# The backward scan's D times x joins the forward sum as a TensorE product with a diagonal matrix, in a two-layer Mamba block

## The chip, the cores and the metric

The kernel runs on one core of one Trainium2 chip. The metric is the device time of one execution in microseconds, here the median of three runs. In the profile the engines are PE (TensorE), DVE (VectorE), ACT (ScalarE), POOL (GpSimd) and SP (SyncE, which issues the DMAs).

## The reference

The input x has 8 images of 96 channels and 32 x 32 places. Two layers follow each other. Each is a Mamba block with 192 inner channels and 16 states; the core of it is

```python
def step(h, inp):
    x_t, dt_t, B_t, C_t = inp
    dA = jnp.exp(dt_t[:, :, None] * A)
    h = dA * h + dt_t[:, :, None] * B_t[:, None, :] * x_t[:, :, None]
    y = jnp.einsum('bds,bs->bd', h, C_t)
    return (h, y)
...
return jnp.swapaxes(ys, 0, 1) + x * D
...
return y * _silu(z) @ W_out
```

where x is the silu of a causal convolution of four taps over an input projection, dt is a softplus, and B and C come from a projection of x. Layer 0 runs it along each row of 32 places and normalises the result over the channels. Layer 1 normalises again and runs it over all 1024 places of an image, once forward and once on the flipped sequence, with the same weights, and adds the two outputs. The gate silu(z) and W_out are the same in both directions, so the kernel adds the two y before the gate. The term x * D occurs in each direction: it is D times the forward x plus D times the backward x, and the two x differ, since the convolutions run opposite ways.

## The kernel before

**Items, tiles, steps.** The images go in four pairs. A pair has three items: ROWS (layer 0), FWD and BWD (layer 1). The 192 channels of two images are three tiles of 128 partitions x 1024 places: tile 0 and tile 1 are the first 128 channels of either image, tile 2 holds the last 64 channels of both. A tile has 16 states, so an item has 48 steps. The twelve items stand in the order ROWS 0, ROWS 1, FWD 0, BWD 0, ROWS 2, FWD 1, BWD 1, ROWS 3, FWD 2, BWD 2, FWD 3, BWD 3, and make 576 steps.

**A step** g works on one state of one tile. ACT computes the decay exp(delta*A) of 128 x 1024 (L616). The input u*B is made in one of two ways: PE spreads a row of B over the partitions into b_ps (L479, `look_ahead`) and DVE multiplies it by u there (L771), with the decay in a_ring; or, for the steps listed in BY_POOL, SP fetches the spread row into b_ring by DMA, POOL multiplies it (L850), and the decay goes into b_ps. DVE then scans (L805) into one of 6 slots of `ring`. POOL multiplies the slot by a row of C that a DMA has spread into c_ring (L856, `product`), and PE adds it to y_ps in PSUM by a product with the identity, half by half (L487, `sum_half`), accumulating over the 16 states. When a tile is summed, DVE's `take` (L785) adds y_ps, half by half, to yv in SBUF.

**Order.** Each engine walks the steps in an order of its own (`walk`): PE ahead, sum_0, jobs, sum_1; ACT the decays ahead, then jobs; DVE take_0, scan, take_1, ahead, jobs; POOL the b product of step g+3, then product g, then jobs; SP the b rows of step g+6, the c rows of step g+3, then jobs. PE's sums run 4 steps late (SUM_LAG), so walk step s sums step s-4, and the scan of step g waits for the sums up to step g-6 (RING). SP's fetch of a b row waits for the scan that read the slot before; b_ring has 2 slots. In `take` a tile is taken at walk step 4 of the next tile.

**Jobs** are the rest of the work, put by hand into slots (the step numbers in PREP, POST, FIRST_BACK and so on), in order on every engine. The preparation of the next item: convolution on PE (xr_first and xr, L534), silu into xs on ACT (L653), the projection dbl on PE (L510), its split into three bf16 parts on ACT and DVE (L665, L666, L673, L830, L834), the DMAs bc_in of SP (L408 to L419), dt on PE with softplus on ACT (L678), and u on POOL (L866, L868). The work behind an item: gated on POOL (L877), w_out on PE, and for ROWS also centre, var, log, rstd, norm (L881) and affine. PE, ACT and DVE hand results over through `bank`, two halves of PSUM of which each has to be emptied before it is used again.

**skip** is the job of the term x * D. For ROWS and FWD, ACT writes xs * D into yv (L656), which starts the sum in SBUF. For BWD the job stands in FWD's steps 14, 16 and 16 (12, 14 and 17 for the first pair, FIRST_BACK), and DVE adds xs * D to FWD's yv with one scalar_tensor_tensor per tile of 128 x 1024 (L824); all its operands lie in SBUF. `take` of the forward tile waits for both signals of skip_done. xs holds the x of one item; the silu of the item after BWD writes over BWD's.

**constants** is a job before the first step: DVE splits the weights of dt, corrects w_out (L754), makes w_centre (L756) and at last negates neg_a (L759), for which PE's next job waits through s_const.

Of the kernel before, what the change touches and what calls it, by code (L numbers as in the profile page):

```python
# [8 lines left out]
B, C, H, W = 8, 96, 32, 32  # L9
T = H * W  # L10
DI = 2 * C
NS = 16
RANK = C // 16
TAPS = 4
P = 128
# [9 lines left out]
TILES = 3  # L25
# [53 lines left out]
SUM_LAG = 4  # L79


def fills_prep(kind, pair, at=None):
# [7 lines left out]
    for k in range(TILES):  # L90
        out.append((at["skip"][k], "skip", k))
# [120 lines left out]
def build_program(nc, x, wpack, out):  # L212
# [6 lines left out]
    with ExitStack() as ctx:  # L219
# [24 lines left out]
        w_centre = sb("w_centre", [C, C])  # L244
        b_centre = sb("b_centre", [C, 1])
        w_sum = sb("w_sum", [P, 2])
        ring = sb("ring", [P, RING, T])
# [4 lines left out]
        neg_a = sb("neg_a", [P, 2, 2 * NS])  # L252
# [10 lines left out]
        ident = col("ident")  # L263
        small = [col("small", l).rearrange("p (m c) -> p m c", m=2) for l in range(2)]
# [195 lines left out]
        def _(pe):  # L460
# [21 lines left out]
            def sum_half(g, j):  # L482
                n = g % NS
                pe.wait_ge(g_ready, g + 1)
                if n == 0:
                    wait(pe, y_taken, 2 * (g // NS - 1) + j + 1)
                nc.tensor.matmul(half(y_ps[:, :], j), ident, half(ring[:, g % RING, :], j),  # L487
                                 start=(n == 0), stop=(n == NS - 1)).then_inc(g_summed, 1)
# [53 lines left out]
            def job(name, kind, pair, i, unit):  # L542
# [44 lines left out]
                elif name == "centre":  # L587
                    pe.wait_ge(norm_done, 4 * pair + k + 1)
                    product(unit, C, [(w_centre[:, :], half(x1[:, k, :], j))])
# [9 lines left out]
        def _(act):  # L599
# [40 lines left out]
            def job(name, kind, pair, i, unit):  # L640
# [3 lines left out]
                if name == "silu":  # L644

                    if ordinal[kind, pair] and j == 0:

                        before = ITEMS[ordinal[kind, pair] - 1]
                        act.wait_ge(K["set_ready"][before["kind"]], 3 * before["pair"] + nth(k))
                    u = unit_for(name, kind, pair, i)  # L650
# [3 lines left out]
                elif name == "skip" and kind != BWD:  # L654
# [58 lines left out]
        def _(dve):  # L713
# [13 lines left out]
            def constants():  # L727
# [28 lines left out]
                nc.vector.tensor_scalar(w_centre[:, :], col("centre")[0:C, :], col("ln")[0:C, 0:1], None, ALU.mult)  # L756
# [16 lines left out]
            def take(tile, j):  # L773
# [3 lines left out]
                if j == 0:  # L777
                    dve.wait_ge(K["skip_done"][kind], 3 * pair + k + 1)
                    if kind == FWD:
                        dve.wait_ge(K["skip_done"][BWD], 3 * pair + k + 1)  # L780
# [32 lines left out]
            def job(name, kind, pair, i, unit):  # L813
# [3 lines left out]
                if name == "constants":  # L817
                    constants()
                elif name == "skip" and kind == BWD:

                    dve.wait_ge(K["skip_done"][FWD], 3 * pair + i + 1)
                    landed(dve, "silu", kind, pair, 2 * i, 2 * i + 1)
                    y = yv_of(kind, pair, i)
                    nc.vector.scalar_tensor_tensor(out=y, in0=xs[:, i, :], scalar=sm[:, m_of(i), 6:7], in1=y,  # L824
# [125 lines left out]
```

## Time and profile before

| | us |
|---|---|
| median of 3 runs | 2148.76 |
| lowest, highest | 2145.57, 2149.55 |
| the profiled execution's own time | 2145.41 |
| its span, first to last instruction | 2143.4 |
| mean granted clock of TensorE | 0.94 of full |

The profile shows one execution. A group by line gives the busy time of all instructions of one line, engine and form. A timeline gives them in order of time, neighbours of one group merged (x4 is four instructions), and in brackets how long the engine was idle before and which instruction ended that; "<-issue" is a wait for nothing that the profile shows. A product of 32-bit numbers stands in the trace as two MATMUL records. Idle time of an engine that sets no pace costs nothing.

### The profile page before, as it was taken

To read this page: it belongs to the slowest core of one execution; us is meant where nothing else is said; L and a number is where in the kernel's file an instruction comes from. 1 tells how busy PE (TensorE), PEld (TensorE's weight loads), DVE (VectorE), ACT (ScalarE), POOL (GpSimd) and SP (SyncE) were. 2 spreads that over 40 slices of the span, in tenths; PEclk is the share of its full clock that TensorE was granted. 3 is DMA by queue.
4 is the path that set the end of the run, shared out by engine and by line. 5 is a ranking of instruction groups with operands and counts; after the bars stand their busy time and mean duration, and the time that the engine had idled before them with its cause. 6 is when DMAs were issued, how large, how long until landed. Compare 5 with 4: busy or idle time off the path is not lost. (4 is left out here: it accounts for less than half of the span.)

```text
span 2143.4 us, 16030 instructions
## 1 busy us (share of the span) xinstructions
PE 1796.1 (84%) x4426; PEld 693.7 (32%) x4426; DVE 1872.9 (87%) x1120; ACT 1163.1 (54%) x1206; POOL 1944.8 (91%) x852
## 2 busy tenths in 40 slices
PE   5797889887898889789889889879879878877777
PEld 2233233332333333233333333323333333223332
DVE  2888887887899988998899997998989998999994
ACT  2756465645746645644756745745575564453331
POOL 0998999888999999998999999899899999899996
PEclk9798999999999999999999989999999999988897
DMA  3567466536575767665665775685566576667673
GB/s 76 207 214 189 162 224 182 168 147 217 152 213 192 215 188 243 191 200 199 199 177 203 236 207 200 203 207 184 190 186 210 199 214 188 221 200 205 229 213 92
DMA packets 124454, 414.99 MB, mean 194 GB/s; under 512 B 18557, under 2 KB 22925, under 8 KB 124365
## 3 DMA queue, kind: packets, MB, share of 16 engines
q1 hardware_dynamic: 124364, 413.98, 63.4%
q8 instruction: 35, 0.57, 0.1%
q14 instruction: 55, 0.44, 0.1%
HBM read 403.48 MB, written 6.29 MB: 191 GB/s over the span
## 5 line engine op out<-in xcount | busy, mean ns | idle before, releaser
L856 POOL TENSOR_TENSOR ring<-ring,c_ring 128x1024 f32<-128x1024 f32 x576 | 1344.6, 2355 | 93.3 <-DVE ring L805 71.7
L487 PE MATMUL y_ps<-ring,wp 128*128 128x512 f32 x2304 | 1175.9, 628 | 48.0 <-DVE yv_fwd L785 25.6
L805 DVE TENSOR_TENSOR_SCAN ring<-a_ring,b_ps 128x1024 f32<-128x1024 f32 x392 | 895.4, 2284 | 32.3 <-ACT a_ring L616 2.3
L487 PEld LDWEIGHTS y_ps<-ring,wp 128*128 128x128 f32 x2304 | 451.0, 200 | 529.9 <-issue 415.3
L805 DVE TENSOR_TENSOR_SCAN ring<-b_ps,b_ring 128x1024 f32<-128x1024 f32 x184 | 417.2, 2273 | 59.3 <-POOL b_ring L850 31.3
L616 ACT ACTIVATE a_ring<-delta_ab,neg_a 128x1024 f32<-128x1024 f32 x240 | 271.8, 1140 | 183.8 <-DVE ring L805 183.2
L850 POOL TENSOR_TENSOR b_ring<-u_ab,b_ring 128x1024 f32<-128x1024 f32 x144 | 343.7, 2387 | 27.3 <-DMA b_ring<-b_rows 27.3
L771 DVE TENSOR_TENSOR b_ps<-u_ab,b_ps 128x1024 f32<-128x1024 f32 x240 | 290.9, 1212 | 79.3 <-PE b_ps L479 72.8
L616 ACT ACTIVATE b_ps<-delta_ab,neg_a 128x1024 f32<-128x1024 f32 x144 | 160.6, 1116 | 238.8 <-DVE ring L805 238.4
L609 ACT ACT_TABLE_LOAD x186 | 238.6, 1283 | 88.2 <-DVE ring L805 36.0
L616 ACT ACTIVATE a_ring<-delta_m,neg_a 128x1024 f32<-128x1024 f32 x152 | 173.6, 1143 | 154.1 <-DVE ring L805 153.8
L479 PE MATMUL b_ps<-b_in,sel 96*128 96x512 bf16 x480 | 154.8, 407 | 94.9 <-DVE ring L805 93.8
L534 PE MATMUL bank<-x,w_conv 96*128 96x512 f32 (+12 forms) x576 | 205.2, 600 | 5.7 <-ACT xs L653 4.5
L771 DVE TENSOR_TENSOR b_ps<-u_m,b_ps 128x1024 f32<-128x1024 f32 x152 | 183.8, 1209 | 15.3 <-PE b_ps L479 15.3
L479 PE MATMUL b_ps<-b_in,sel_m 96*128 96x512 bf16 x304 | 98.8, 408 | 115.8 <-DVE ring L805 115.6
L479 PEld LDWEIGHTS b_ps<-b_in,sel 96*128 96x128 bf16 x480 | 42.3, 102 | 259.4 <-DVE ring L805 149.9
L534 PEld LDWEIGHTS bank<-x,w_conv 96*128 96x128 f32 (+1 forms) x576 | 71.6, 163 | 126.9 <-issue 112.2
L479 PEld LDWEIGHTS b_ps<-b_in,sel_m 96*128 96x128 bf16 x304 | 24.6, 104 | 235.2 <-DVE ring L805 189.4
L850 POOL TENSOR_TENSOR b_ring<-u_m,b_ring 128x1024 f32<-128x1024 f32 x40 | 95.2, 2380 | 2.1 <-DMA b_ring<-b_rows 2.1
L616 ACT ACTIVATE b_ps<-delta_m,neg_a 128x1024 f32<-128x1024 f32 x40 | 44.7, 1117 | 96.2 <-DVE ring L805 96.2
L534 PE MATMUL bank<-io,w_conv 96*128 96x512 f32 (+5 forms) x192 | 67.0, 596 | 13.8 <-DMA io<-x 13.4
L868 POOL TENSOR_TENSOR u_ab<-delta_ab,xs 128x1024 f32<-128x1024 f32 x8 | 18.8, 2350 | 55.1 <-ACT delta_ab L678 55.1
(76 smaller groups left out, 967.8 us busy)
## 6 DMA issues: line engine op xcount, KB each, us to landing
c_ring<-c_rows SPq DMA_DIRECT2D x384, 512.0 KB, 4.9
c_ring<-c_rows SPq DMA_DIRECT2D x384, 256.0 KB, 4.3
b_ring<-b_rows SPq DMA_DIRECT2D x144, 512.0 KB, 5.2
b_ring<-b_rows SPq DMA_DIRECT2D x80, 256.0 KB, 5.2
out<-io SPq DMA_DIRECT2D x16, 192.0 KB, 5.2
io<-x SPq DMA_DIRECT2D x6, 384.0 KB, 7.1
b_in<-parts SPq DMA_DIRECT2D x36, 64.0 KB, 2.0
dt_in<-parts SPq DMA_DIRECT2D x72, 24.0 KB
```

What stands on the lines that cost most here:

```text
L479: last = nc.tensor.matmul(half(b_ps[:, g % 2, :], j), pick(k, n), half(b_in[:, parity(kind, pair), :], j), start=True, stop=True)
L487: nc.tensor.matmul(half(y_ps[:, :], j), ident, half(ring[:, g % RING, :], j), start=(n == 0), stop=(n == NS - 1)).then_inc(g_summed, 1)
L534: last = nc.tensor.matmul(o, w, m, start=(d == 0), stop=(d == TAPS - 1))
L609: nc.scalar.preload_act_table_set(name)
L616: nc.scalar.activation(dst, delta_of(kind, pair, k), ACT.Exp, scale=neg_a[:, LAYER[kind], m_of(k) * NS + n:m_of(k) * NS + n + 1]).then_inc ...
L771: nc.vector.tensor_tensor(b, u_of(kind, pair, k), b, ALU.mult).then_inc(b_used, 1)
L805: nc.vector.tensor_tensor_scan(out=h, data0=a, data1=b, initial=0.0, op0=ALU.mult, op1=ALU.add).then_inc(h_ready, 1)
L850: nc.gpsimd.tensor_tensor(b, u_of(kind, pair, k), b, ALU.mult).then_inc(b_made, 1)
L856: nc.gpsimd.tensor_tensor(r, r, c_ring[:, g % C_RING, :], ALU.mult).then_inc(g_ready, 1)
L868: nc.gpsimd.tensor_tensor(u, d, xs[:, i, :], ALU.mult).then_inc(u_done, 1)
```

## The change

The DVE job skip for BWD is gone. In its place DVE makes, once among the constants, two matrices of 128 x 128 with D of layer 1 on the diagonal (w_skip). In every FWD tile PE multiplies them with the backward xs, half by half, and accumulates into y_ps ahead of the sum of state 10 (SKIP_AT), that is at walk steps 14, 30 and 46 of the item. `take` waits for ACT's part alone. ACT's silu of the item after BWD waits, tile by tile, for the sums of the forward tile, since these now read the backward xs. To make room, w_centre and neg_a lie in the packed weights wp and are written in place; DVE waits for PE's product of `constants` before it writes over w_centre.

```diff
--- before.py
+++ after.py
@@ -77,6 +77,7 @@
 LEAD = {"ahead": 1, "ahead_c": C_LEAD, "ahead_a": 2, "ahead_a2": 1, "ahead_b": 3}
 SP_LEAD = dict(LEAD, ahead_b=B_LEAD)
 SUM_LAG = 4
+SKIP_AT = 10
 
 
 def fills_prep(kind, pair, at=None):
@@ -87,8 +88,9 @@
         out.append((at["xr"][u], "xr_first", u))
         out.append((at["xr"][u] + 1, "xr", u))
         out.append((at["silu"][u], "silu", u))
-    for k in range(TILES):
-        out.append((at["skip"][k], "skip", k))
+    if kind != BWD:
+        for k in range(TILES):
+            out.append((at["skip"][k], "skip", k))
     for j in range(2):
         for n, name in enumerate(("dbl", "split_hi", "split_mid", "split_lo")):
             out.append((at["dbl"][j] + n, name, j))
@@ -241,15 +243,14 @@
         parts3 = sb("parts3", [SPLIT_ROWS, 2, 3, HALF], bf16)
         dt_in = sb("dt_in", [DT_ROWS, T], bf16)
         w_dt = sb("w_dt_parts", [DT_ROWS, 2, 3, P], bf16)
-        w_centre = sb("w_centre", [C, C])
         b_centre = sb("b_centre", [C, 1])
         w_sum = sb("w_sum", [P, 2])
+        w_skip = sb("w_skip", [P, 2, P])
         ring = sb("ring", [P, RING, T])
         c_ring = sb("c_ring", [P, C_RING, T])
         a_ring = sb("a_ring", [P, A_RING, T])
         b_ring = sb("b_ring", [P, B_RING, T])
         eps = sb("eps", [C, 1])
-        neg_a = sb("neg_a", [P, 2, 2 * NS])
         b_ps = ps("b_ps", [P, 2, T])
         y_ps = ps("y_ps", [P, T])
         bank = ps("bank", [P, 2, HALF])
@@ -261,6 +262,9 @@
             return wp[:, at:at + n]
 
         ident = col("ident")
+        w_centre = col("centre")[0:C, :]
+        at = _cols["a_log", 0][0]
+        neg_a = wp[:, at:at + 4 * NS].rearrange("p (l n) -> p l n", l=2)
         small = [col("small", l).rearrange("p (m c) -> p m c", m=2) for l in range(2)]
         ordinal = {(it["kind"], it["pair"]): n for n, it in enumerate(ITEMS)}
         parity = lambda kind, pair: ordinal[kind, pair] % 2
@@ -484,6 +488,10 @@
                 pe.wait_ge(g_ready, g + 1)
                 if n == 0:
                     wait(pe, y_taken, 2 * (g // NS - 1) + j + 1)
+                kind, pair, k, _ = step_at(g)
+                if kind == FWD and n == SKIP_AT:
+                    landed(pe, "silu", BWD, pair, 2 * k + j)
+                    nc.tensor.matmul(half(y_ps[:, :], j), w_skip[:, m_of(k), :], half(xs[:, k, :], j), start=False, stop=False)
                 nc.tensor.matmul(half(y_ps[:, :], j), ident, half(ring[:, g % RING, :], j),
                                  start=(n == 0), stop=(n == NS - 1)).then_inc(g_summed, 1)
 
@@ -586,7 +594,7 @@
                                       (w[own, C:2 * C], half(yv_of(kind, pair, 2), j)[own, :])])
                 elif name == "centre":
                     pe.wait_ge(norm_done, 4 * pair + k + 1)
-                    product(unit, C, [(w_centre[:, :], half(x1[:, k, :], j))])
+                    product(unit, C, [(w_centre, half(x1[:, k, :], j))])
                 elif name == "var":
                     c = i % 4
                     landed(pe, "w_out" if i < 4 else "centre", kind, pair, c)
@@ -647,11 +655,13 @@
 
                         before = ITEMS[ordinal[kind, pair] - 1]
                         act.wait_ge(K["set_ready"][before["kind"]], 3 * before["pair"] + nth(k))
+                        if before["kind"] == BWD:
+                            act.wait_ge(g_summed, 2 * NS * (TILES * ordinal[FWD, before["pair"]] + k + 1))
                     u = unit_for(name, kind, pair, i)
                     src = full(u)
                     table("silu_and_others")
                     empty(u, nc.scalar.activation(half(xs[:, k, :], j), src, ACT.Silu, bias=sm[:, m_of(k), 4:5]))
-                elif name == "skip" and kind != BWD:
+                elif name == "skip":
                     landed(act, "silu", kind, pair, 2 * i, 2 * i + 1)
                     nc.scalar.activation(yv_of(kind, pair, i), xs[:, i, :], ACT.Identity,
                                          scale=sm[:, m_of(i), 6:7]).then_inc(K["skip_done"][kind], 1)
@@ -724,7 +734,7 @@
             dve.wait_ge(taps_in, 16)
             fold(1)
 
-            def constants():
+            def constants(unit):
                 nc.vector.tensor_copy(sel[:, :, :], col("sel")[0:C, :].rearrange("p (b n) -> p b n", b=2)).then_inc(s_sel, 1)
                 dve.wait_ge(s_sel, 1)
                 for b in range(2):
@@ -753,7 +763,10 @@
                 for v in range(2):
                     last = nc.vector.tensor_scalar(wo[:, v, :], wo[:, v, :], w_sum[:, v:v + 1], None, ALU.add)
                 last.then_inc(s_sums, 1)
-                nc.vector.tensor_scalar(w_centre[:, :], col("centre")[0:C, :], col("ln")[0:C, 0:1], None, ALU.mult)
+                for m in range(2):
+                    nc.vector.tensor_scalar(w_skip[:, m, :], ident, small[1][:, m, 6:7], None, ALU.mult)
+                dve.wait_ge(produced[unit % 2], unit // 2 + 1)
+                nc.vector.tensor_scalar(w_centre, w_centre, col("ln")[0:C, 0:1], None, ALU.mult)
                 dve.wait_ge(s_sums, 3)
                 dve.wait_ge(s_nega, 2)
                 last = nc.vector.tensor_scalar(neg_a[:, :, :], neg_a[:, :, :], -1.0, None, ALU.mult)
@@ -775,9 +788,8 @@
                 it = ITEMS[tile // TILES]
                 kind, pair, k = it["kind"], it["pair"], tile % TILES
                 if j == 0:
-                    dve.wait_ge(K["skip_done"][kind], 3 * pair + k + 1)
-                    if kind == FWD:
-                        dve.wait_ge(K["skip_done"][BWD], 3 * pair + k + 1)
+                    if kind != BWD:
+                        dve.wait_ge(K["skip_done"][kind], 3 * pair + k + 1)
                     if kind == BWD:
                         dve.wait_ge(y_taken, 2 * (tile - TILES + 1))
                 dve.wait_ge(g_summed, 2 * NS * (tile + 1) - 1 + j)
@@ -815,14 +827,7 @@
                 k, j = i // 2, i % 2
                 sm = small[layer]
                 if name == "constants":
-                    constants()
-                elif name == "skip" and kind == BWD:
-
-                    dve.wait_ge(K["skip_done"][FWD], 3 * pair + i + 1)
-                    landed(dve, "silu", kind, pair, 2 * i, 2 * i + 1)
-                    y = yv_of(kind, pair, i)
-                    nc.vector.scalar_tensor_tensor(out=y, in0=xs[:, i, :], scalar=sm[:, m_of(i), 6:7], in1=y,
-                                                   op0=ALU.mult, op1=ALU.add).then_inc(K["skip_done"][kind], 1)
+                    constants(unit)
                 elif name == "split_hi":
                     u = unit_for("dbl", kind, pair, i)
                     dve.wait_ge(K["hi_ready"][kind], 2 * pair + i + 1)
```

## Rows read from the trace of the kernel before

**Rows 1.** The page's first part: busy us, share of the span and xinstructions

```profile
PE 1796.1 (84%) x4426; PEld 693.7 (32%) x4426; DVE 1872.9 (87%) x1120; ACT 1163.1 (54%) x1206; POOL 1944.8 (91%) x852
```

**Rows 2.** Groups by line: xcount | busy us, mean ns | idle before, releasers

```profile
L824 DVE SCALAR_TENSOR_TENSOR yv_fwd<-xs,wp,yv_fwd 128x1024 f32<-128x1024 f32 x9 | 33.5, 3733 | 0.0
...
L824 DVE SCALAR_TENSOR_TENSOR yv_rows<-xs,wp,yv_rows 128x1024 f32<-128x1024 f32 x3 | 13.1, 4392 | 0.0
```

**Rows 3.** Timelines of F3: start us, us, instruction [idle before <-releaser]

```profile
1842.30 10.66 DVE L824 SCALAR_TENSOR_TENSOR yv_rows<-xs,wp,yv_rows 128x1024 f32<-128x1024 f32 x1
...
1855.66 2.27 DVE L805 TENSOR_TENSOR_SCAN ring<-b_ps,b_ring 128x1024 f32<-128x1024 f32 x1
...
1846.38 1.88 PE L487 MATMUL y_ps<-ring,wp 128*128 128x512 f32 x4
...
1862.79 2.41 POOL L850 TENSOR_TENSOR b_ring<-u_ab,b_ring 128x1024 f32<-128x1024 f32 x1 [5.20 <-DMA b_ring<-b_rows]
```

**Rows 4.** Timeline of DVE in F0

```profile
459.70 10.31 DVE L824 SCALAR_TENSOR_TENSOR yv_fwd<-xs,wp,yv_fwd 128x1024 f32<-128x1024 f32 x1
```

**Rows 5.** Timeline of POOL in F0

```profile
466.61 2.33 POOL L850 TENSOR_TENSOR b_ring<-u_ab,b_ring 128x1024 f32<-128x1024 f32 x1
472.30 2.35 POOL L856 TENSOR_TENSOR ring<-ring,c_ring 128x1024 f32<-128x1024 f32 x1 [3.36 <-DVE ring L805]
478.55 2.40 POOL L850 TENSOR_TENSOR b_ring<-u_ab,b_ring 128x1024 f32<-128x1024 f32 x1 [3.91 <-DMA b_ring<-b_rows]
```

**Rows 6.** Timelines of PE, ACT, DVE and POOL in F1

```profile
997.55 4.45 PE L487 MATMUL y_ps<-ring,wp 128*128 128x512 f32 x10
...
998.72 1.10 ACT L616 ACTIVATE b_ps<-delta_ab,neg_a 128x1024 f32<-128x1024 f32 x1
...
991.41 6.98 DVE L824 SCALAR_TENSOR_TENSOR yv_fwd<-xs,wp,yv_fwd 128x1024 f32<-128x1024 f32 x1
...
1001.09 2.27 DVE L805 TENSOR_TENSOR_SCAN ring<-b_ps,b_ring 128x1024 f32<-128x1024 f32 x1
...
1007.37 2.38 POOL L850 TENSOR_TENSOR b_ring<-u_ab,b_ring 128x1024 f32<-128x1024 f32 x1 [4.35 <-DMA b_ring<-b_rows]
```

**Rows 7.** Timeline of PE in F0

```profile
463.03 1.94 PE L534 MATMUL bank<-x,w_conv 96*64 96x512 f32 x8
...
472.27 1.03 PE L479 MATMUL b_ps<-b_in,sel 96*128 96x512 bf16 x2 [6.25 <-DVE ring L805]
...
474.94 2.93 PE L534 MATMUL bank<-x,w_conv 96*64 96x512 f32 x8
```

**Rows 8.** Stretches: length, busy us (x) of PE, PEld, DVE, ACT, POOL, PEclk, DMA

```profile
472.30:477.80 5.50, 5.50 (x12) 1.53 (x12) 5.50 (x4) 1.12 (x1) 2.34 (x1) 0.57 0.42 116
1054.60:1059.80 5.20, 5.20 (x7) 1.76 (x8) 2.28 (x1) 3.14 (x6) 5.20 (x3) 0.50 0.26 84
...
985.00:1012.00 27.00, 23.72 (x55) 8.16 (x54) 24.78 (x14) 12.50 (x20) 19.29 (x10) 1.00 0.44 152
```

**Rows 9.** Timelines around step 30: F1 (PE, POOL), F0, F2 and F3

```profile
1058.09 1.91 PE L487 MATMUL y_ps<-ring,wp 128*128 128x512 f32 x2
...
1075.49 2.36 POOL L856 TENSOR_TENSOR ring<-ring,c_ring 128x1024 f32<-128x1024 f32 x1 [0.20 <-DVE ring L805]
...
555.49 1.23 DVE L771 TENSOR_TENSOR b_ps<-u_m,b_ps 128x1024 f32<-128x1024 f32 x1 [1.92 <-PE b_ps L479]
...
1580.38 9.28 POOL L856 TENSOR_TENSOR ring<-ring,c_ring 128x1024 f32<-128x1024 f32 x4
...
1906.62 0.60 PE L479 MATMUL b_ps<-b_in,sel_m 96*128 96x512 bf16 x2 [2.99 <-DVE ring L805]
```

**Rows 10.** Timeline of PE near step 46 of F1

```profile
1109.39 0.61 PE L479 MATMUL b_ps<-b_in,sel_m 96*128 96x512 bf16 x2 [1.18 <-DVE ring L805]
```

**Rows 11.** Timeline of PE before the first step, and a group by line

```profile
51.64 1.01 PE L510 MATMUL bank<-dt_in,w_dt_parts 72*128 72x512 bf16 x2 [7.01 <-DVE neg_a L759]
...
L754 DVE TENSOR_SCALAR wp<-wp,w_sum 128x96 f32<-128x96 f32 x2 | 0.4, 268 | 0.0
```

## Prediction

> **What bounds the kernel now.** I read the page first: no engine idles much. POOL is busy 91%, DVE 87%, PE 84% [rows 1]. So the share of busy time decides nothing, and the question is which engine sets the pace in each stretch. I call the twelve items R0, R1, F0, B0, R2, F1, B1, R3, F2, B2, F3, B3 in their order (R rows, F forward, B backward). The removed instruction runs in F0, F1, F2 and F3, at steps 12 to 17.
>
> The groups by line [rows 2] show how odd it is. Twelve additions at L824 keep DVE busy for 33.5 + 13.1 = 46.6 us. The group on yv_rows has three, 13.1 us, and one of them takes 10.66 us [rows 3], so the other two take 1.22 us each. Hence 12 x 1.22 = 14.6 us is work, and 32.0 us is time in which the instruction has started and does not finish. It comes to a long hold on the first addition of each F item (10.31, 6.98 and 10.66 us in F0, F1 and F3 [rows 3, 4, 6]; F2 repeats F1) and a short one on one more in F0.
>
> The timelines of F0 show what holds it. DVE starts L824 at 459.70 and is held until 470.01 [rows 4]. POOL multiplies back to back, and the last of four begins at 466.61 and ends at 468.94 [rows 5]; the addition ends 1.07 us later, about one undisturbed duration. In F1 and F3 it is the same. L824 is the only instruction of the steady loop by which DVE reads two tensors of SBUF; scans, products and L785 have one operand in PSUM. I read this as a path into SBUF that DVE's second operand shares with POOL, and that DVE gets only once POOL has run dry.
>
> Then POOL starves in turn: 3.36 us until DVE's next scan, and 3.91 us for a row of b_ring, which SP may fetch only after a scan has freed the slot [rows 5]. F1 has 4.35 us for the second wait [rows 6], F3 5.20 us [rows 3], F2 lies between.
>
> The Trainium skill (SBUF — State Buffer, Who interferes with whom) has the rule: a DVE instruction with two SBUF inputs contends with a GpSimd instruction that reads SBUF, and the one that issues first keeps the shared pair for its whole instruction. The trace agrees on the pair, and not on the length: by the rule a hold ends with the multiplication then running, 2.4 us at most, where F0's lasts 9.1 us, almost four of them.
>
> **Removed: L824, twelve times.** On DVE at most 46.6 us goes. How much of it reaches the end depends on what is late next, and that is PE. sum_1 of a step stands behind the jobs of its slot in PE's order, and scan g waits for sum g-6.
>
> *F0.* PE idles for 6.25 us until 472.27 [rows 7], waiting for the scan behind the held addition. It then works on at a granted clock of 0.57, mostly the lower level of 1.2 GHz [rows 8]: a broadcast and a sum fill the 2.67 us from 472.27 to 474.94, of which half, 1.3 us, is owed to the clock, and the convolution of eight records takes 2.93 us where the one at 463.03 takes 1.94: 1.0 us. Without the hold PE goes straight on, and its own work sets the pace of the scans behind it. Gain 6.25 + 2.3 = 8.55 us, less the added products of this step.
>
> *F1, F2.* Here PE never stopped before the hold was over: between 985 and 1012 it is busy 23.72 of 27.00 us at clock 1.00 [rows 8]. Step 14 has two w_out and one dbl, and sum_1(10) starts only at 997.55 [rows 6]. Scan 16 needs this sum. So the 6.98 us of hold lie beside PE's work, and scan 16, now at 1001.09, can move only as far as PE allows.
>
> *F3.* Only one w_out precedes: sum_1(10) starts at 1846.38, while scan 16 starts at 1855.66 [rows 3]. PE has more than 8 us of slack.
>
> **Added: 24 products.** Each stands in a trace as two MATMUL records, as the five sums do that make the row of ten at 997.55: 4.45 us, 0.44 a record [rows 6]. A forward tile gets four, 1.8 us, at steps 14, 30 and 46 of an F item, all twelve tiles 21 us (42 us at half the clock).
>
> *Tile 0.* Both go ahead of sum_1(10). F0: 8.55 - 1.8 = 6.8 us gain. F1: sum_1(10) ends at 997.55 + 1.8 + 1.0 = 1000.3; the decay for scan 16, which ran at 998.72 for 1.10 us behind the copies of dbl [rows 6], comes 0.9 later and ends at 1000.7. Scan 16 starts there and not at 1001.09: 0.4 us. The next row of b_ring follows the scan's end by a fixed time, and POOL, which is busy from 1007.37 on without a break of note, moves by the same 0.4. F2 likewise 0.4. F3: the sum ends at 1846.38 + 1.8 + 1.0 = 1849.2, the decay with it at about 1849.6; scan 16 moves from 1855.66 by 6.1 us, and POOL's wait for b_ring, which ends at 1862.79 [rows 3], by as much. Sum 6.8 + 0.4 + 0.4 + 6.1 = 13.7 us.
>
> *Tile 1.* In F1 PE works at clock 0.50 before the broadcast of step 32 [rows 8]; the product ahead of sum_1(26) costs 0.86 a record there (the sum at 1058.09 takes 1.71 us for two until the broadcast at 1059.80). The other stands ahead of an idle stretch and is free. DVE waits for that broadcast, and POOL already waits 0.20 for DVE at 1075.49 [rows 9]: a cost of 1.8 us. In F0 DVE waits 1.92 for the broadcast at 555.49, behind two products: 1.8 us too. In F2 the last of the four products from 1580.38 on starts at 1587.3, 2 us after its scan: covered. In F3 PE idles 2.99 us right before: covered. Were these covers gone, 1.8 us each.
>
> *Tile 2.* PE idles 1.18 us in each of the steps around 46 [rows 10]; of the 1.8 us 0.6 may reach the next broadcast, for which DVE has room. I take nothing, at most 4 x 0.6 us.
>
> **Moved and new waits.** PE's wait for silu, behind which stand sums, jobs and broadcasts, is for work at least six steps old and holds nothing; at worst a silu runs late by one table load and 0.7 us, which no row suggests. ACT's silu behind a backward item waits for the sums of a tile that ended at least eight steps before; queued behind it are decays, and I price it at nothing. take no longer waits for the additions, whose signals are never late. No DMA is added or moved.
>
> **Start.** Two scalings of 128x128 stand on DVE ahead of neg_a, for which PE waits 7.01 us until 51.64 and behind which the first scan hangs [rows 11]. The nearest row is L754 with 268 ns for 96 columns, of which two overlap a little: 0.25 us each, 0.5 us in all, bounds 0.3 and 1.0. DVE's new wait there, for the product that makes b_centre, is for one already done, with nothing but the rest of the constants behind it. neg_a and w_centre in wp change places only.
>
> **Sum.** 13.7 - 3.6 - 0.5 = 9.6 us less, against the profiled execution's own time of 2145.4 us: 2135.8. That execution lies 3.4 us below the median of 2148.8, so the forecast is 2139.2 us.
>
> **Rivals.**
>
> *POOL sets the pace, and gets all its idle time back.* 4 x 3.36 + 3.91 + 4.35 + about 4.7 + 5.20 = 31.6 us. For it: POOL is the busiest engine. Against: in F1 and F2 POOL's second wait hangs on scan 16, that on sum_1(10), and PE has no room. Less 3.6 and 0.5: 2121 us. Chance 0.17. (All 46.6 us of DVE would give 2106; nothing speaks for it.)
>
> *Given back later.* In F0 PE waits for dt_in at step 27. If that transfer were due at a time of its own, F0's gain would be lost, and 2.8 us stay: 2146. Against: SP issues it behind a wait on POOL's products, so it should move along. Chance 0.10.
>
> *The hold is not POOL's doing and stays.* If one multiplication of 2.4 us is POOL's part and the rest lands on the next DVE instruction, F0 keeps 10.31 - 1.22 - 2.4 = 6.7 us of hold and F3 7.0 us, which is their gain; 0.8 - 3.6 - 0.5 makes 3.3 us more, 2152. Against: four holds end with POOL's last multiplication. Chance 0.06. The Trainium skill's rule named above (same page and section), by which a hold cannot outlast one instruction, gives this case.
>
> *Slower: PE's backlog at steps 30 and 46.* There the added records stand ahead of broadcasts for which DVE waits. Eight tiles x four records x 0.86 us at half the clock are 27.5 us; all on the path, against 13.7 gained, make 14.3 us more, 2163. It decides from 13.2 of the 27.5 us on. For it: the clock of 0.50 at step 30. Against: PE's idle time around step 46, and the covers in F2 and F3. Chance 0.07.
>
> **Numbers.** The forecast's chance is 0.60, its own range 2131 to 2144. 0.2%, about what a measurement of this kernel can tell from no change, is 4.3 us. Faster 0.60 + 0.17 = 0.77; within it 0.10 + 0.05 of the staying hold = 0.15; slower 0.08. The range 2120 to 2147 takes in the first three cases and leaves out about 0.13.
>
> **What would show it.** DVE busy some 46 us less and no L824; 24 products of w_skip; POOL's pair of waits near step 15 gone from F0, its first wait shorter than 3.4 us in F3, and still 6 to 7 us in all in F1 and F2; PE without the idle 6.25 us in F0. F0 and F3 shorter by 5 to 6 us each, F1 longer by 1, F2 unchanged. I am wrong if POOL's idle time in F1 or F2 falls by over 4 us (then PE was not the limit), if some other DVE instruction is held for several us, or if DVE's waits for the broadcasts grow by over 10 us.

## The result, and the profile after

The changed kernel takes 2133.3 us (median of 4 runs, 2129.02 to 2136.97), the kernel before 2147.2 us over 4 runs (2145.57 to 2149.55). The ratio is 0.9941, 95% interval 0.9919 to 0.9963: 12.7 us less by the ratio, where 9.6 were forecast. Two repetitions of the same pair, in the experiments, give 0.9948 and 0.9936. The time lies in the range and on the side forecast. The profiled execution has a span of 2135.0 us and a time of its own of 2136.97 us, 8.4 less than that of before on either count.

The page's first part after (busy us, share, xinstructions; against [rows 1]):

```profile
PE 1814.8 (85%) x4474; PEld 705.1 (33%) x4474; DVE 1829.8 (86%) x1110; ACT 1162.8 (54%) x1206; POOL 1938.6 (91%) x852
```

DVE is busy 43.1 us less. The additions' 46.6 us went and 0.5 for two scalings came; no other group of DVE moved by over 0.2 us. The other 3 us are overlap: the page counts time in which two neighbouring instructions overlap once, and the durations added up one by one fall by 45.8 us. PE is busy 18.7 us more. That is 48 new records, which the groups by line show (xcount | busy us, mean ns | idle before), with the scalings beneath. Their 26.4 us count the overlap with the rows beside them: two records are 1.02 us long in the timeline below, and the next row starts after 0.86.

```profile
L494 PE MATMUL y_ps<-xs,w_skip 128*128 128x512 f32 x48 | 26.4, 633 | 0.0
...
L767 DVE TENSOR_SCALAR w_skip<-wp 128x128 f32<-128x128 f32 x2 | 0.5, 278 | 0.0
```

**F0.** The timeline of PE (start us, us, instruction), where [rows 7] had an idle 6.25 us:

```profile
466.11 0.60 PE L483 MATMUL b_ps<-b_in,sel 96*128 96x512 bf16 x2
466.55 1.02 PE L494 MATMUL y_ps<-xs,w_skip 128*128 128x512 f32 x2
467.41 1.02 PE L495 MATMUL y_ps<-ring,wp 128*128 128x512 f32 x2
468.36 1.94 PE L542 MATMUL bank<-x,w_conv 96*64 96x512 f32 x8
470.22 1.13 PE L494 MATMUL y_ps<-xs,w_skip 128*128 128x512 f32 x2
471.19 1.88 PE L495 MATMUL y_ps<-ring,wp 128*128 128x512 f32 x4
473.00 1.93 PE L542 MATMUL bank<-x,w_conv 96*64 96x510 f32 x8
```

PE goes from one item to the next without a gap, and the granted clock is 1.00 where it was 0.57 behind the idle stretch [rows 8]; the convolution of eight records takes 1.93 us and not 2.93 (the row of the stretch: length, then busy us of PE, PEld, DVE, ACT, POOL, clock, DMA share, GB/s):

```profile
466.10:474.00 7.90, 7.90 (x27) 2.83 (x27) 5.17 (x3) 3.51 (x4) 7.90 (x4) 1.00 0.58 194
```

POOL, which in [rows 5] waited 3.36 and 3.91 us here, multiplies from 460.15 to 492.7 with no wait. And the scan behind the second product now waits for the sum, so PE sets the pace, as the forecast had it (timeline of DVE):

```profile
472.34 2.29 DVE L817 TENSOR_TENSOR_SCAN ring<-b_ps,b_ring 128x1024 f32<-128x1024 f32 x1 [1.92 <-PE y_ps L495]
```

**F1 and F3.** The timelines of F1, first PE, then ACT, DVE and POOL:

```profile
991.58 2.82 PE L518 MATMUL bank<-xs,wp 128*96 128x512 f32 x6
994.23 1.02 PE L494 MATMUL y_ps<-xs,w_skip 128*128 128x512 f32 x2
995.09 4.46 PE L495 MATMUL y_ps<-ring,wp 128*128 128x512 f32 x10
...
994.43 0.59 ACT L675 ACTIVATE x_out<-bank 96x512 f32<-96x512 f32 x1 [1.67 <-PE bank L518]
994.92 0.58 ACT L676 ACTIVATE parts<-bank 44x512 bf16<-44x512 f32 x1
995.40 2.14 ACT L624 ACTIVATE b_ps<-delta_ab,wp 128x1024 f32<-128x1024 f32 x2
...
995.53 0.69 DVE L835 TENSOR_TENSOR bank<-bank,parts 44x512 f32<-44x512 f32 x1 [5.83 <-ACT parts L676]
996.54 4.47 DVE L817 TENSOR_TENSOR_SCAN ring<-b_ps,b_ring 128x1024 f32<-128x1024 f32 x2 [0.31 <-ACT b_ps L624]
...
1003.09 2.35 POOL L855 TENSOR_TENSOR b_ring<-u_ab,b_ring 128x1024 f32<-128x1024 f32 x1 [7.95 <-DMA b_ring<-b_rows]
```

The 6.98 us of hold [rows 6] have turned into 5.83 us of waiting. PE comes to dbl behind two w_out, ACT copies its result at 994.43, the decay follows at 995.40 and the scan at 996.54. POOL's two idle stretches, 3.36 + 4.35 = 7.7 us, have become one of 7.95. In F3, where one w_out less precedes:

```profile
1843.89 0.69 DVE L835 TENSOR_TENSOR bank<-bank,parts 44x512 f32<-44x512 f32 x1 [3.77 <-ACT parts L676]
1844.89 2.29 DVE L817 TENSOR_TENSOR_SCAN ring<-b_ps,b_ring 128x1024 f32<-128x1024 f32 x1 [0.31 <-ACT b_ps L624]
...
1852.00 2.35 POOL L855 TENSOR_TENSOR b_ring<-u_ab,b_ring 128x1024 f32<-128x1024 f32 x1 [2.91 <-DMA b_ring<-b_rows]
```

POOL idles 2.91 us here and not 3.36 + 5.20 [rows 3].

The items' lengths, each from its first scan to the first scan of the next, and in brackets the start of scan 16 behind the item's first (worked out from the starts of the scans in each trace, us; the kernels of the columns are told below; after_again is the changed kernel a second time):

```
      before        after         after_again   no_product    add_from_psum  add_late
F0  194.3 (65.1)  189.9 (58.1)  192.4 (58.1)  185.7 (56.4)  187.1          189.5
F1  182.3 (65.5)  181.8 (65.1)  180.7 (65.1)  179.0 (64.2)  178.0          187.1 (64.8)
F2  179.3 (65.3)  179.6 (65.1)  180.0 (65.1)  177.9 (64.2)  180.2          186.4 (64.2)
F3  178.4 (69.1)  171.9 (63.0)  171.9 (63.0)  171.3 (62.4)  171.3          179.3
```

The four F items are 11.1 us shorter together, more than the 8.4 us of the span: R0 and B3, which the change doesn't touch, are 1.8 and 2.9 us longer in this trace (B3 from its first scan to the end of its last). From trace to trace of all kernels R0 lies between 168 and 170.5 us, R1 between 184.8 and 190.1, B3 between 150 and 153.9.

The traces show where this comes from: the granted clock falls to its lower level in short stretches, and these don't lie at the same steps in each trace. In B3 the same six records of PE's sums, behind the same wait for `take`, take 2.81 us before and 5.46 after; then DVE waits for the broadcast behind them, as it did not before (PE before, PE after, DVE after):

```profile
1979.77 2.81 PE L487 MATMUL y_ps<-ring,wp 128*128 128x512 f32 x6 [1.68 <-DVE yv_rows L785]
...
1968.59 5.46 PE L495 MATMUL y_ps<-ring,wp 128*128 128x512 f32 x6 [1.68 <-DVE yv_rows L797]
...
1974.71 1.23 DVE L784 TENSOR_TENSOR b_ps<-u_ab,b_ps 128x1024 f32<-128x1024 f32 x1 [1.65 <-PE b_ps L483]
```

Scans 4 to 8 of B3 take 15.5 us with a clock of 1.00 before, and 17.4 us with 0.80 after; 17.2 and 17.3 in the two repetitions of the changed kernel. In R1, the stretch from scan 6 to 10 takes 16.3 us in every trace with at most 2.1 us at the lower level there, 19.4 and 19.5 in the two with 6.8, and 20.9 and 21.0 in the two with 10.2. Whether the change itself moves these stretches, or chance does, no run here decides. So one item carries an uncertainty of 2 to 5 us by where they fall, and only scan starts close behind an item's first are sharp, most of them to 0.1 us and some to 0.7.

### The profile page after: what moved, and what is told of

Read it like the earlier page. It is cut to its first block and busy times, and to the rows that moved or that the text cites. A ratio compares the mean times of both kernels' runs of the same rounds, so it can differ in the third digit from the quotient of the medians.

```text
span 2135.0 us, 16128 instructions
## 1 busy us (share of the span) xinstructions
PE 1814.8 (85%) x4474; PEld 705.1 (33%) x4474; DVE 1829.8 (86%) x1110; ACT 1162.8 (54%) x1206; POOL 1938.6 (91%) x852
## 5 line engine op out<-in xcount | busy, mean ns | idle before, releaser
L624 ACT ACTIVATE a_ring<-delta_ab,wp 128x1024 f32<-128x1024 f32 x240 | 271.8, 1140 | 183.7 <-DVE ring L817 183.2
L624 ACT ACTIVATE b_ps<-delta_ab,wp 128x1024 f32<-128x1024 f32 x144 | 160.4, 1115 | 213.0 <-DVE ring L817 212.6
L624 ACT ACTIVATE a_ring<-delta_m,wp 128x1024 f32<-128x1024 f32 x152 | 173.6, 1143 | 155.0 <-DVE ring L817 154.7
L784 DVE TENSOR_TENSOR b_ps<-u_m,b_ps 128x1024 f32<-128x1024 f32 x152 | 183.8, 1209 | 20.5 <-PE b_ps L483 20.5
L624 ACT ACTIVATE b_ps<-delta_m,wp 128x1024 f32<-128x1024 f32 x40 | 44.7, 1117 | 95.0 <-DVE ring L817 94.9
```

What stands on the lines that cost most here:

```text
L624: nc.scalar.activation(dst, delta_of(kind, pair, k), ACT.Exp, scale=neg_a[:, LAYER[kind], m_of(k) * NS + n:m_of(k) * NS + n + 1]).then_inc ...
L784: nc.vector.tensor_tensor(b, u_of(kind, pair, k), b, ALU.mult).then_inc(b_used, 1)
```

## The experiments

The runs were made in three groups, each with runs of the kernel before of its own (medians 2145.6, 2147.1 and 2146.2 us); the ratios are against all of these in a group. My theory: the hold is a wait of DVE's second SBUF operand for POOL; what it costs is decided by PE's order of work; the products cost PE about 10 us. The rivals were that the hold costs little anywhere because POOL or a transfer is late regardless; that POOL's idle time is what was won; that the products are free.

### The changed kernel again, twice

> The changed kernel as it is, for a comparison on the same chip. If the first measurement (ratio 0.9941) holds, 11 to 14 us less than the kernel before. F0 about 4.5 us shorter, F3 about 6.5 us, F1 and F2 within 1 us of before.

Measured: 2133.62 us, ratio 0.9948 (0.993 to 0.9965). Scan 16 starts at the same 0.1 us in all four F items as in the first trace. Against before, F3 is 6.5, F0 1.9 and F1 1.6 us shorter and F2 0.7 longer, so F0 and F1 miss what was expected of them. Behind scan 16 of F0 the clock is at its lower level for 27.3 us here and for 20.5 in the first trace.

> The changed kernel as it is, for a comparison with the next three on the same chip. 10 to 14 us less than the kernel before.

Measured: 2133.52 us, ratio 0.9936 (0.9921 to 0.9951). Scan 16 starts at the same 0.1 us in F0 and F2, and 0.6 and 0.2 us later in F1 and F3. Against before, F0 is 4.1, F1 1.6 and F3 6.3 us shorter, F2 1.8 longer.

### The change without its products

```diff
                 if kind == FWD and n == SKIP_AT:
                     landed(pe, "silu", BWD, pair, 2 * k + j)
-                    nc.tensor.matmul(half(y_ps[:, :], j), w_skip[:, m_of(k), :], half(xs[:, k, :], j), start=False, stop=False)
```

> The changed kernel with the 24 products of w_skip left out, so D times the backward x is missing from y. Theory (PE sets the pace at tile 0 of every F item and at tile 1 of F0 and F1): 1.8 us less at tile 0 in each of four items and 1.8 us less at tile 1 in F0 and F1, 10 to 11 us less than the changed kernel, some 23 us less than the kernel before. Rival, PE's products lie beside other work: within 3 us of the changed kernel. Rival, POOL sets the pace everywhere: the same as the changed kernel too, and POOL's idle time in F1 and F2 unchanged.

Measured: 2122.91 us, ratio 0.9891 (0.9866 to 0.9916), which is 10.7 us under the changed kernel: the size expected in sum. The scans say where. At tile 0, scan 16 is 1.7 us earlier in F0 (both products, 1.8 forecast), 0.9 in F1 and F2, 0.6 in F3: there only the product ahead of dbl was in the way, not the second. At tile 1 the lead over the changed kernel grows between scans 28 and 32 by 2.2 us in F0 (from 111.3 - 109.7 = 1.6 to 132.5 - 128.7 = 3.8), and in the same way by 1.6 in F1, 0.8 in F2 and 0.1 in F3. Taken against the two repetitions of the changed kernel it is 1.3 and 2.4 in F0, 1.4 and 0.0 in F1, -0.2 and 0.7 in F2, -0.3 and 0.2 in F3: so far out, the price by item isn't sharp.

### The addition kept, its second operand taken from PSUM

```diff
+    skip = at["skip"] if kind != BWD or at is not PREP else (14, 14, 17)
...
-                    nc.vector.scalar_tensor_tensor(out=y, in0=xs[:, i, :], scalar=sm[:, m_of(i), 6:7], in1=y,
...
+                    dve.wait_ge(b_used, dve_before[g] + 1)
+                    nc.vector.scalar_tensor_tensor(out=y, in0=xs[:, i, :], scalar=sm[:, m_of(i), 6:7], in1=b_ps[:, g % 2, :],
```

> The kernel before, with DVE's addition reading its second operand from b_ps in PSUM instead of yv in SBUF, at steps 14, 14, 17 (so yv gets D times x plus a wrong tile; length, place and count of the instruction are kept). Theory (the hold is a wait for the path into SBUF that POOL uses): no hold, twelve instructions of 1.2 to 1.3 us, DVE busy 32 us less at this line, F0 and F3 shorter by 5 to 7 us each, the whole 9 to 13 us less than before, since DVE's remaining 15 us lie beside PE's and POOL's work. Rival, the hold comes from the instruction itself or its scalar operand: holds of 7 to 11 us stay, and the time is that of before.

Measured: 2121.98 us, ratio 0.9902 (0.9876 to 0.9929). The groups by line of this kernel:

```profile
L828 DVE SCALAR_TENSOR_TENSOR yv_fwd<-xs,wp,b_ps 128x1024 f32<-128x1024 f32 x9 | 11.3, 1279 | 0.9
L828 DVE SCALAR_TENSOR_TENSOR yv_rows<-xs,wp,b_ps 128x1024 f32<-128x1024 f32 x3 | 3.8, 1279 | 0.3
```

Against [rows 2], the same instruction of the same size, takes 15.1 us in place of 46.6. Each of the twelve overlaps a multiplication of POOL, and none is held, nor is any of these multiplications longer than 2.53 us. This shows that the second SBUF operand is what is held. POOL's side was not varied by a run; that it is POOL that holds it rests on the timing, told in the last section. The gain is larger than expected: I had left out that this kernel also doesn't pay for the products, which by the run above are worth 10.7 us. It stands level with the kernel without them.

### The held addition moved to where PE has room

```diff
+    skip = at["skip"] if kind != BWD else (22, 24, 26)
...
-                    if kind == FWD:
-                        dve.wait_ge(K["skip_done"][BWD], 3 * pair + k + 1)
```

> The kernel before, with DVE's three additions of an F item at steps 22, 24 and 26, where PE has slack, and take no longer waiting for them. Theory (in F1 and F2 the hold costs nothing because PE is the limit around step 14): the hold of the first addition stays at 5 to 11 us, now in F1 and F2 too on the path, which become 5 to 8 us longer; F0 and F3 gain at step 14 what they lose at step 22; the whole 8 to 16 us more than before. Rival, a hold costs the same wherever it stands: within 3 us of before.

Measured: 2153.58 us, ratio 1.004 (1.0025 to 1.0055). Timelines of DVE and POOL in F1:

```profile
1018.73 7.14 DVE L823 SCALAR_TENSOR_TENSOR yv_fwd<-xs,wp,yv_fwd 128x1024 f32<-128x1024 f32 x1
1031.49 1.26 DVE L823 SCALAR_TENSOR_TENSOR yv_fwd<-xs,wp,yv_fwd 128x1024 f32<-128x1024 f32 x1
1039.48 2.48 DVE L823 SCALAR_TENSOR_TENSOR yv_fwd<-xs,wp,yv_fwd 128x1024 f32<-128x1024 f32 x1
...
1022.46 2.33 POOL L855 TENSOR_TENSOR ring<-ring,c_ring 128x1024 f32<-128x1024 f32 x1
1028.15 2.35 POOL L855 TENSOR_TENSOR ring<-ring,c_ring 128x1024 f32<-128x1024 f32 x1 [3.36 <-DVE ring L804]
```

A hold of 7.1 us, as long as the 6.98 at step 14, makes F1 4.8 and F2 7.1 us longer than in the kernel before; F3 is 0.9 longer. Scan 16 is 0.7 and 1.1 us earlier than there; scan 24 starts at 98.9 and 98.2 us, not 94.5 and 94.4. So the same hold is for the most part hidden beside PE's pile at step 14 and costs about its length a few steps later. The place decides, not the DVE time. F0 goes the other way, 4.8 us shorter; its hold is only 2.65 us there, which I take for the reason.

### Two w_out of F1 and F2 at steps 16 and 17, with and without the change

```diff
-POST = {ROWS: dict(gated=(2, 2, 7), w_out=(13, 13, 14, 14), var=(20, 22, 23, 23, 32, 33, 33, 34),
+POST = {ROWS: dict(gated=(2, 2, 7), w_out=(13, 13, 16, 17), var=(20, 22, 23, 23, 32, 33, 33, 34),
```

> The changed kernel with two of the four w_out of F1 and F2 moved from step 14 to steps 16 and 17, which takes 3.5 us of PE's work out from before sum_1(10). Theory (PE's order sets scan 16 in F1 and F2): each of the two items 2 to 3.5 us shorter, the whole 4 to 7 us less than the changed kernel. Rival (POOL or the fetch of b_ring sets the pace there): F1 and F2 within 1 us of the changed kernel.

Measured: 2131.27 us, ratio 0.9935 (0.9911 to 0.9959). Scan 16 starts 4.1 us earlier in F1 and F2 (61.0): PE's order sets it, shown. The items are only 1.3 and 1.6 us shorter than in the second trace of the changed kernel, less than the 2 to 3.5 expected: steps 18 to 20 now take 10.6 us in place of 7.1. R1, which has none of the moved work, is 5.0 us longer in this trace, with one of the long stretches of lower clock told above.

> The kernel before with the same move of two w_out. Theory (here the hold and PE's work end scan 15 and sum 10 at nearly the same time, so relieving PE alone gives nothing): F1 and F2 within 1 us of before, the whole within 3 us. Rival (PE alone is the limit in F1 and F2, the hold is wholly hidden): the same gain as in the changed kernel, 4 to 7 us.

Measured: 2157.96 us, ratio 1.0062 (1.0037 to 1.0087): a miss, as within 3 us of before was expected and 10.9 more came (2147.1 in the same group). F2 has what was expected: hold of 6.93 us, scan 16 unmoved (65.4). But the moved product meets a bank that DVE has not yet read (timeline of PE in F1), and the steps 18 to 20 take 13.7 us in F1 and 14.6 in F2, where the kernel before took 6.7 in both:

```profile
1010.03 3.94 PE L510 MATMUL bank<-yv_rows,wp 128*96 128x512 f32 x4 [3.83 <-DVE parts L834]
```

And in F1 the addition was held for one multiplication only. Timelines of DVE and POOL:

```profile
996.34 2.29 DVE L824 SCALAR_TENSOR_TENSOR yv_fwd<-xs,wp,yv_fwd 128x1024 f32<-128x1024 f32 x1
...
995.13 2.41 POOL L856 TENSOR_TENSOR ring<-ring,c_ring 128x1024 f32<-128x1024 f32 x1
997.49 3.38 POOL L850 TENSOR_TENSOR b_ring<-u_ab,b_ring 128x1024 f32<-128x1024 f32 x1
```

The items come out at 182.0 us in F1 (0.3 shorter than before) and 187.6 in F2 (8.3 longer); R1, which has none of the moved work, is 4.5 longer, with 10.2 us of lower clock where the kernel before has 0.6. The pair of runs therefore doesn't separate hold from PE's order by the whole time. The starts of scan 16 do: with the two w_out out of the way it starts 4.1 us earlier without the hold (changed kernel, F1 and F2), 4.7 earlier with a hold of 2.3 us (F1 here, at 60.8), and 0.1 later with one of 6.9 us (F2 here). So in the kernel before, the hold and PE's work both stand right ahead of scan 16 in F1 and F2, and taking away either alone brings little: nothing in F2 here, and 0.4 and 0.2 us in the changed kernel, 1.3 and 1.1 without its products.

### The addition into PSUM when the tile is taken

In the changed kernel, PE's products and w_skip are left out, and DVE adds D*xs to y_ps just ahead of take, 24 additions of 128x512 and none to y in SBUF (an excerpt):

```diff
+                    nc.vector.scalar_tensor_tensor(out=half(y_ps[:, :], j), in0=half(xs[:, k, :], j),
+                                                   scalar=small[1][:, m_of(k), 6:7], in1=half(y_ps[:, :], j),
+                                                   op0=ALU.mult, op1=ALU.add).then_inc(K["skip_done"][BWD], 1)
```

> The changed kernel without PE's products: DVE adds D times the backward x to y_ps in PSUM, half by half, right before take reads it (one operand in SBUF, one in PSUM, 24 instructions of about 0.67 us on DVE). Theory (what cost time was the second SBUF operand, not DVE's work): no hold, 20 to 24 us less than before, 8 to 12 less than the changed kernel, like add_from_psum. Rival, DVE is near its limit and 16 us of its work count: no better than the changed kernel. A risk for both: PE's first sum of the next tile waits for take, which comes 0.7 us later on each half.

Measured: 2139.84 us over 10 runs, ratio 0.9965 (0.9951 to 0.9979). A miss: it is faster than before, by 7.5 us, and not faster than the change. Nothing is held (24 instructions, 17.7 us in all), but against the kernel with the operand from PSUM F0 is 2.6, F1 2.1 and F3 3.6 us longer, F2 0.3 shorter. DVE's 0.74 us stands between a tile's last sum and the next tile's first, twice a tile. That this is the whole of the difference I have not tried.

### The products at other steps

SKIP_AT says at which sum of a tile the products stand.

```diff
-SKIP_AT = 10
+SKIP_AT = 13
```

> The changed kernel with the products at steps 17, 33 and 49. Theory (they cost 1.8 us where they stand ahead of a sum or a broadcast that is due): in F1, F2 and F3 they no longer delay sum 10; 2 to 6 us less than the changed kernel. Rival, the cost is PE's work as such, wherever it stands: within 1.5 us of the changed kernel.

Measured: 2138.41 us over 10 runs, ratio 0.9961 (0.9943 to 0.9978). A miss. The near part holds: scan 16 starts 1.7 us earlier in F0 and 0.9 in F1 and F2, as without any product. The F items end as late as in the changed kernel, so the same work of PE costs as much three steps later; B0, B1 and B2 are 0.8, 1.0 and 0.3 us longer than in its first trace. The time lies 4.9 us above that of the changed kernel in other groups, but the intervals of the ratios overlap: it isn't shown to be slower.

```diff
-SKIP_AT = 10
+SKIP_AT = (10, 6, 3)
...
-                if kind == FWD and n == SKIP_AT:
+                if kind == FWD and n == SKIP_AT[k]:
```

> The changed kernel with the product of tile 1 at step 26 and that of tile 2 at step 39, where PE had 3 to 4 us of idle time in four steps. Theory (a product costs time only where PE is late): F0 2 us shorter (its tile 1 product stood ahead of the broadcast of step 32), F1 up to 1.5 us, scan 16 of every F item unmoved; 2 to 4 us less than the changed kernel. Rival (a product costs wherever it stands): no change.

Measured: 2136.21 us, ratio 0.9957 (0.9941 to 0.9974). F0 is 1.9 us shorter than in the changed kernel's trace of the same group (after_third), as expected, and F1 and F2 are not: no gain that can be told from the changed kernel.

### One w_out later, and both moves

```diff
-POST = {ROWS: dict(gated=(2, 2, 7), w_out=(13, 13, 14, 14), var=(20, 22, 23, 23, 32, 33, 33, 34),
+POST = {ROWS: dict(gated=(2, 2, 7), w_out=(13, 13, 14, 15), var=(20, 22, 23, 23, 32, 33, 33, 34),
```

> The changed kernel with one of the four w_out of F1 and F2 at step 15 instead of 14, as F3 has it, so that no w_out waits for the bank that dbl holds. Theory (PE's order sets scan 16): scan 16 starts 1.7 to 2 us earlier in F1 and F2, and the items end 1 to 2 us earlier; 2 to 4 us less than the changed kernel. Rival (another wait takes its place before the item ends): scan 16 earlier, items unchanged.

Measured: 2132.75 us, ratio 0.9935 (0.992 to 0.9951). Scan 16 starts at 63.0 us in F1 and F2, 2.1 earlier, which is the price of one w_out at full clock (4.10 us for two). Against the changed kernel's trace of the same group F1 is 1.5 and F2 3.0 us shorter, R1, which has none of the moved work, 3.2 longer. The kernel's time can't be told from the changed one's.

> Both moves together. Theory: their gains add, 4 to 7 us less than the changed kernel, 15 to 20 us less than the kernel before. Rival: as the changed kernel.

Its diff is that of w_out=(13, 13, 14, 15) and that of SKIP_AT = (10, 6, 3) together. Measured: 2130.67 us, ratio 0.9922 (0.9905 to 0.994): the lowest of the versions that compute the whole, 2.9 us under the changed kernel of the same group, but the intervals overlap. It isn't shown to be better.

## Why the prediction was right

**The hold's nature** was read rightly in the main. It goes with the second SBUF operand (twelve of twelve), and the rival in which it stays and lands elsewhere is false: no other DVE instruction is held (the longest scan or product of DVE takes 2.29 us after, as before). That DVE gets the path only once POOL has run dry was too strong: in seven of 18 cases DVE gets in behind a single multiplication and POOL goes on, and the short hold of 3.12 us in F0 of the kernel before is one of them.

**Tile 0** was right almost to the number. Scan 16 against the item's first moved by -7.0, -0.4, -0.2 and -6.1 us in F0 to F3; the forecast was -6.8, -0.4, -0.4 and -6.1. In F1 the reason was only partly right. I charged both products and let the scan start with a decay that ended at 1000.7. The trace without products shows that one, 0.9 us, is in the way, because the scan's chain is dbl, ACT's copies and the decay, not sum_1(10): the decay starts at 995.40, while the sum behind the second product runs from 995.09 for 0.9 us.

**POOL's idle time** in F1 and F2 did not fall (7.7 to 7.95 us in F1, 8.2 in F2), so the rival in which POOL gets it all back is out, and the test I set for it, a fall of over 4 us, was not met.

**What tile 0 left out** is the step that failed, though the sum came out near. I counted the hold and not the two other additions, of which the forecast had written 1.22 us each. In F1 and F2 they stand between scans 16 and 17 (timeline of DVE in F1, kernel before):

```profile
1003.29 2.44 DVE L824 SCALAR_TENSOR_TENSOR yv_fwd<-xs,wp,yv_fwd 128x1024 f32<-128x1024 f32 x2
1005.66 2.27 DVE L805 TENSOR_TENSOR_SCAN ring<-b_ps,b_ring 128x1024 f32<-128x1024 f32 x1
```

After, the two scans are one row of 4.47 us (996.54, above): scan 17 comes 2.7 us earlier against the item's first and not 0.4, scan 20 still 2.0 in F1 and 1.6 in F2. POOL's wait in F1 nevertheless ends where it did (71.8 us behind the item's first scan before, 71.7 after), so this lead is DVE's alone. It is 1.3 us at scan 28 and 0.1 at scan 32 (1.2 in both repetitions): most or all of it is used up where the products of tile 1 come. I charged these 1.8 us to F1's end, and F1 ended 0.5 us shorter (1.6 in both repetitions), where 1.4 longer was forecast. In F0, where the third addition had a short hold, scan 18 comes 9.9 us earlier, but scan 20 again 7.0 as scan 16 does: nothing of it reached the end. So what failed in F1 and F2 is the term for the moved path: 0.4 us each for scan 16, with the 2.4 us of the other two additions taken as worth nothing; they were worth 2.3 us at scan 17 and had partly or wholly melted by scan 32.

**Tile 1** was sized about right in sum. Against the run without products the first trace prices it at 2.2, 1.6, 0.8 and 0.1 us in F0 to F3, together 4.7, where I had 1.8, 1.8, 0 and 0, together 3.6; the two repetitions give 2.2 and 3.3 in all. The one in F3 is covered, as forecast; for F2 the three traces don't agree. In F0 DVE waits for the broadcasts behind the products, as [rows 9] had 1.92 for one of them (timeline of DVE in F0, after):

```profile
545.35 1.23 DVE L784 TENSOR_TENSOR b_ps<-u_m,b_ps 128x1024 f32<-128x1024 f32 x1 [2.10 <-PE b_ps L483]
...
551.33 1.23 DVE L784 TENSOR_TENSOR b_ps<-u_m,b_ps 128x1024 f32<-128x1024 f32 x1 [2.38 <-PE b_ps L483]
```

Its lead over before falls from 7.1 us at scan 28 to 4.8 at scan 32 and 4.4 at the end. F2 moves by +0.3, +0.7 and +1.8 us in the three traces, F3 by -6.5, -6.5 and -6.3.

**The other rivals.** "Given back later" is false for dt_in: PE's two waits for it in F0 are 20.1 us before and after, its first dt product starts 6.8 us earlier, and the item stayed 4.4 us shorter (1.9 and 4.1 in the repetitions). The rival is true in small for the products, through the broadcasts. The slower rival, PE's backlog at tiles 1 and 2, exists at a quarter of its price: all products cost 10.7 us, tile 0's 4.1 of them (1.7 + 0.9 + 0.9 + 0.6), which leaves 6.6 of 27.5, and the point from which it decides was 13.2. The waits of DVE for broadcasts, for which I had set 10 us as a limit, grew by 13.8 (88.1 to 101.9) in the first trace. That sign of failure went off, and the forecast stood all the same. In the two repetitions they are 91.8 and 90.0 us, and of the 13.8 only 8.4 lie in F items (19.1, 15.9, 11.6 and 3.0 against 14.5, 14.2, 10.4 and 2.1). I had set the limit without knowing how much this sum varies between traces of one kernel.

**The sum.** The F items give 11.1, 9.3 and 10.2 us less in three traces, where 13.7 - 3.6 = 10.1 was forecast. The start was priced at 0.5; the two scalings take 0.5 of busy time and the stretch up to the first scan is 0.9 us shorter. The profiled execution was to take 2135.8 us and took 2137.0. The median lies 5.9 us under the forecast, for another reason: I added 3.4 us because the profiled execution before lay that much below its median, and the one after lies 3.7 above its own (3.4 + 3.7 - 1.2 = 5.9). So the near hit of the median rests in part on luck. Why the medians differ by 2 to 3 us more than the F items do stays open; untouched items vary by as much with the stretches of lower clock.

## What to carry to other kernels

An instruction that is several times longer than its equals in the trace may be held and not at work: look at which operand of it, and which engine beside it, differs from its quick equals, and change that operand's memory. What a hold costs depends on what is late beside it. Against the kernel with neither additions nor products, the additions from step 14 on cost F1 and F2 3.3 and 1.4 us, and those from step 22 on, with the same hold, 8.1 and 8.5. Measure a kernel twice before you set a bound on a sum of waits, and before you read a difference of 2 us in an item, look whether the granted clock was the same at the same steps.

## What the runs showed of the hardware

DVE's addition with two SBUF operands against POOL's multiplications had these outcomes in three kernels (before, the late additions, and w_out moved without the change). With POOL idle at its start it takes 1.25 to 1.27 us; where POOL begins a multiplication meanwhile (four cases of the late additions), that one takes 3.30 to 3.31 us in place of 2.35. Or it gets in behind the one multiplication that runs (2.3 to 3.1 us), and then POOL's next takes 3.33 to 3.38 us in place of 2.35. Or it lasts through three to five multiplications, the one that runs at its start counted, and ends about 1.1 us after the last, with POOL dry (6.9 to 11.0 us). POOL then waits 3.36 us, each time. The long outcome came in eleven cases, each with POOL at work back to back for at least three multiplications before; the middle one in six cases with at most one such, and once, at 996.34 in the experiment above, with 21 of them. Behind that one, two more additions took 1.25 and 1.27 us inside a single multiplication, which then took 5.03. What decides between the two is open; it isn't the moment within POOL's multiplication, since the late additions that start 0.93 to 0.96 us into one have the long outcome three times and the middle one four times.

The Trainium skill (SBUF — State Buffer, Who interferes with whom) has contention between the two engines for a shared path, and the pair of outcomes with one multiplication agrees with it. A hold through several multiplications, up to five in these traces, does not follow from it, and here the measurement decides.
